# A transformer block's attention on 1 core: row tiles for scores and maxima, two head groups per sum, key masks made by GpSimd

## What is computed

```python
scores = einsum('bqhd,bkhd->bhqk', q, k) * 8 ** -0.5
out = einsum('bhqk,bkhd->bqhd', softmax(scores, axis=-1), v)
```

## Time and profile before

| | us |
|---|---|
| median of 3 runs | 498.83 |
| the profiled execution | 499.31 |
| its span, first to last instruction | 497.5 |
| PE busy | 428.4 (86%) |
| DVE busy | 351.3 (71%) |
| ACT busy | 289.2 (58%) |
| POOL busy | 61.4 (12%) |
| first score matmul starts | 61.85 |

### The profile page before, as it was taken

One profiled execution on the slowest core, in us unless ns is written; L12 is line 12 of the kernel. 1 busy time (PEld: TensorE's weight loads), 2 busy tenths in 40 slices (PEclk: granted clock), 3 DMA queues, 4 the chain that ended last, 5 costly groups with the idle time before them and its releaser, 6 DMA issues.

```text
span 497.5 us, 10420 instructions
## 1 busy us (share of the span) xinstructions
PE 428.4 (86%) x3664; PEld 271.1 (54%) x3664; DVE 351.3 (71%) x938; ACT 289.2 (58%) x535; POOL 61.4 (12%) x74
## 2 busy tenths in 40 slices
PE   0466699999999989889979989999999998989886
PEld 0433355656666664555545545656566665746464
DVE  4979477888888973875966948997979895531331
ACT  1022177666666666476665575656566667677552
POOL 5711010103021210210011001010101102020130
PEclk9989599999999999999999999999999999999989
DMA  8727475552746543323425136256546463510001
GB/s 256 268 64 212 146 218 138 175 138 84 195 162 171 164 131 107 92 80 113 96 83 165 42 118 152 81 154 194 135 147 154 137 184 113 116 38 24 1 1 42
DMA packets 34410, 63.30 MB, mean 127 GB/s; under 512 B 5535, under 2 KB 9887, under 8 KB 34079
## 3 DMA queue, kind: packets, MB, share of 16 engines
q1 hardware_dynamic: 34071, 62.42, 43.7%
q10 hardware_dynamic: 288, 0.21, 0.1%
HBM read 31.81 MB, written 26.74 MB: 118 GB/s over the span
## 4 chain that ended last, share of the span: by engine, by line
PE 61%; DVE 21%; DMA 5%; issue 4%; ACT 3%; POOL 3%; SPq 2%; DVEq 0%; ACTq 0%
PE ps_max L910 10%; PE ps_ao L942 9%; PE ps_sc L930 9%; PE ps_misc L892 8%; DVE maxima L680 7%; PE ps_misc L987 5%; PE ps_misc L967 5%; PE ps_misc L950 4%; DVE xn L584 4%; PE ps_misc L854 4%; DVE stats L574 3%; PE ps_misc L973 3%; POOL rstd L739 2%; DMA Kd<-Kh 2%; PE ps_misc L899 2%
## 5 line engine op out<-in xcount | busy, mean ns | idle before, releaser
L680 DVE TENSOR_REDUCE maxima<-ps_max 128x4 f32<-128x512 f32 (+1 forms) x256 | 159.7, 665 | 54.7 <-PE ps_max L910 47.4
L824 ACT ACTIVATE PT<-ps_sc 128x512 f32<-128x512 f32 (+1 forms) x256 | 138.9, 596 | 66.9 <-PE ps_sc L930 65.3
L910 PE MATMUL ps_max<-Kd,Qh 128*128 128x512 f32 (+1 forms) x256 | 105.1, 479 | 15.0 <-DMA Kd<-Kh 9.7
L930 PE MATMUL ps_sc<-Qd,Ks 97*128 97x512 f32 (+1 forms) x256 | 93.5, 444 | 0.9 <-issue 0.9
L942 PE MATMUL ps_ao<-PT,V 120*9 120x128 f32 (+1 forms) x2048 | 80.0, 274 | 0.3
L910 PEld LDWEIGHTS ps_max<-Kd,Qh 128*128 128x128 f32 x256 | 44.5, 195 | 51.5 <-issue 19.6
L942 PEld LDWEIGHTS ps_ao<-PT,V 120*9 120x9 f32 (+1 forms) x2048 | 43.3, 90 | 38.2 <-issue 33.5
L736 POOL TENSOR_SCALAR vareps<-mv 128x4 f32<-128x4 f32 (+1 forms) x28 | 6.4, 229 | 414.8 <-DVE mv L577 414.8
L930 PEld LDWEIGHTS ps_sc<-Qd,Ks 97*128 97x128 f32 (+1 forms) x256 | 44.5, 187 | 17.1 <-issue 9.9
L811 ACT ACTIVATE xnT<-ps_misc,vec 128x128 f32<-128x128 f32 x80 | 30.1, 460 | 35.2 <-PE ps_misc L854 18.8
L892 PE MATMUL ps_misc<-xnT,W 128*128 128x512 f32 x72 | 37.8, 639 | 6.4 <-ACT xnT L811 6.4
(11 more groups left out here) (74 smaller groups left out, 441.6 us busy)
## 6 DMA issues: line engine op xcount, KB each, us to landing
Qd<-q_mem SPq DMA_DIRECT2D x128, 96.0 KB
k_mem<-Kh SPq DMA_DIRECT2D x16, 512.0 KB, 2.9
q_mem<-Qh SPq DMA_DIRECT2D x16, 512.0 KB, 2.9
Ks<-k_mem SPq DMA_DIRECT2D x8, 768.0 KB, 7.1
Ks<-k_mem SPq DMA_DIRECT2D x8, 720.0 KB, 6.6
k_mem<-Kl SPq DMA_DIRECT2D x16, 256.0 KB, 3.2
q_mem<-Ql SPq DMA_DIRECT2D x16, 256.0 KB, 3.3
Kd<-Kh SPq DMA_DIRECT2D x128, 16.0 KB
```

What stands on the lines that cost most here:

```text
L680: dve.tensor_reduce(dst, ps_max[:, st.k % MAX_BANKS, 0:HG * ns].rearrange("p (h k) -> p h k", h=HG), AX_X, ALU.max, negate=True).then_inc( ...
L824: act.activation(PT[0:ns, st.k % 4, :], ps_sc[0:ns, st.k % 2, :], ACT.Exp, scale=SCALE).then_inc(S["probs_ready"], 1)
L910: pe.matmul(ps_max[:, st.k % MAX_BANKS, 0:HG * ns], Qh[:, st.f % 2, st.b * P:(st.b + 1) * P], Kd[:, HG * st.n:HG * st.n + HG, st.b * ns:(s ...
L930: pe.matmul(ps_sc[0:ns, st.k % 2, :], Ks[:, st.f % 2, st.n, st.b * ns:(st.b + 1) * ns], Qd[:, half % 3, st.n % GP, :, st.b * P:(st.b + 1) ...
```

## The change

- **Maxima** go by batch: one step makes the scores of the four head groups with four matmuls of 32 rows and 512 (480) columns, one in each row tile. `Kd[:, c]` holds the keys with the rows of the c-th head of every group, the rest zero, and has two slots. POOL makes it with four multiplications of `Kh` by a column of ones and zeros (`head_rows`, which DVE makes once with a sum over the identity); the DMAs and memsets of `Kd` are gone. `ps_max` is gone: the four products take four banks of `ps_misc`, now of 5 banks. The maxima of a unit are turned by one transpose in place of four.
- **Scores** go by two cells (groups 2g and 2g+1 of a batch): `Ks` and `Qd` have four blocks of 32 rows (24, a row for the maximum, 7 unused). Each row tile of 64 rows holds two heads; its matmul has 57 rows and 256 columns. Four such matmuls fill both banks of `ps_sc`, one for each row tile, so PE waits before each step until the exponentials of the step before are done (`probs_ready`, `GP * st.k`). `Qd` has two slots of a unit. ACT takes two exponentials of 512 columns for a step, as before.
- **Sums** of the two cells go to the same 128 columns: weights of 18 columns, with the head's values in the first 9 for the even group and in the last 9 for the odd, added up. A bank holds the sums of half a unit: 2 copies, 2 groups of 4 transposes, 2 reciprocals (of 32 in place of 16 elements) and 4 multiplications (of 128 in place of 64) for a unit.
- **Loads**: the keys come with 4 DMAs in place of 1, the queries with 4 in place of 8 (of twice the size), the maxima with 4 in place of 2.
- **Memsets** on POOL: `V` 3456 elements for each row in place of 1728, and its ones; `Ks` and two of `Qd`, of 4096 each, in place of four of 4096. DVE waits for the constants (`small_in`) before its first statistics.
- **The table `T`** is changed throughout: the first norm at -36.9 in place of -41.92, `value` (4.0, 3.57, 4.26, 5.04) in place of (2.15, 2.16, 2.1, 2.55), and so on. `EARLY` is [0.82, -3.59, -1.1, 0.1] in place of [-0.6, 1.18, 0.4, 0].

```diff
-SROWS = HG * SR
+TROWS = 32
+E = 2
+PAIRS = NG // 2 * CB
 FF = 4
-BANKS = 3
-MAX_BANKS = 2
+BANKS = 5
+ROWS = HG * HD
 VW = HD + 1
+PAIR = 2 * VW
+VSLOTS = 3
+PSLOTS = 4
...
-        for h in range(H):
-            at(t + T["kmask"][a] + h // HG * T["kstep"][a], Step("kmask", h=h, **who))
-        for i in range(period):
-            at(t + T["max"][a] + i // 2 * 2 * T["mstep"][a], Step("max", n=i // CB, b=i % CB, **who))
+        at(t + T["kmask"][a], Step("kmask", **who))
+        for b in range(CB):
+            at(t + T["max"][a] + NG * b * T["mstep"][a], Step("max", b=b, **who))
...
+        for i, (g, b) in enumerate(pairs):
+            at(t + 2 * i, Step("score", b=b, g=g, **who))
+            at(t + i // 2 * 4 + T["value"][a], Step("value", b=b, g=g, **who))
+        for g in range(GP):
+            at(t + 2 * CB * (g + 1) + T["copy"][a], Step("copy", g=g, **who))
+            at(t + 2 * CB * (g + 1) + T["norm"][a], Step("norm", g=g, **who))
...
-        Kd = sb("Kd", [P, H, CT], F32R)
-
-
-        Ks = sb("Ks", [SROWS + 1, 2, NG, CT], F32R)
-        Qd = sb("Qd", [SROWS + 1, 3, GP, HG, CT], F32R)
-        V = sb("V", [P, 3, CB, H, VW])
-        maxima = sb("maxima", [P, CB, H])
-        maxT = sb("maxT", [H, CT], F32R)
-        PT = sb("PT", [P, 4, CT])
...
+        Kd = sb("Kd", [P, 2, HG, CT], F32R)
+        head_rows = sb("head_rows", [P, HG])
+        Ks = sb("Ks", [P, 2, NG, CT], F32R)
+        Qd = sb("Qd", [P, 2, NG, E, CT], F32R)
+        V = sb("V", [P, VSLOTS, CB, H, PAIR])
+        maxima = sb("maxima", [P, H, CB])
+        maxT = sb("maxT", [H * CB, P], F32R)
+        PT = sb("PT", [P, PSLOTS, GP, GP, E, P])
...
-        ps_max = ctx.enter_context(nc.psum_tensor("ps_max", [P, MAX_BANKS, CT], F32))
...
-                        sp.dma_start(f32(Kd[r, st.h, 0:n]),
-                                     f32(Kh[r, st.f % 2, 0:n])).then_inc(S[f"kd_in{st.h // HG}"], 16)
...
-                        sp.dma_start(f32(Ks[0:SROWS, st.f % 2, :, 0:n]),
-                                     k_mem[st.f].rearrange("(n r) s t -> (r s) n t", n=NG)[:, :, 0:n]
-                                     ).then_inc(S[f"keys_in{st.f % 2}"], 16)
...
+                        heads = k_mem[st.f].rearrange("(n c r) s t -> c (r s) n t", n=NG, c=HG)
+                        for c in range(HG):
+                            sp.dma_start(f32(Ks[TROWS * c:TROWS * c + SR, st.f % 2, :, 0:n]),
+                                         heads[c][:, :, 0:n]).then_inc(S[f"keys_in{st.f % 2}"], 16)
...
+                            sp.dma_start(f32(Qd[TROWS * c:TROWS * c + SR, st.f % 2, :, c % E, :]),
+                                         heads[c]).then_inc(S[f"queries_in{st.f % 2}"], 16)
...
+                        heads = m_mem[st.f].rearrange("(n c a) t -> c a n t", n=NG, c=HG)
+                        for c in range(HG):
+                            row = TROWS * c + SR
+                            sp.dma_start(f32(Qd[row:row + 1, st.f % 2, :, c % E, :]),
+                                         heads[c]).then_inc(S[f"maxima_in{st.f % 2}"], 16)
...
+                dve.wait_ge(S["small_in"], 48)
+                dve.tensor_reduce(head_rows[:, :], ident.rearrange("p (n c d) -> p c n d", n=NG, c=HG), AX_XY,
+                                  ALU.add).then_inc(S["rows_ready"], 1)
...
-                            for g in range(2):
-                                dve.memset(f32(Kd[:, g * GH:(g + 1) * GH, :]), 0.0).then_inc(S["zeros_ready"], 1)
-                                if g == 0:
-                                    modulation()
+                            modulation()
...
-                        dve.wait_ge(S["max_scores"], st.k + 1)
-                        dst = maxima[:, st.b, HG * st.n:HG * st.n + HG]
-                        if st.n == 0 and st.b == 0 and st.f:
+                        if st.b == 0 and st.f:
                             dve.wait_ge(S["misc_filled"], mT_use[st.f - 1] + 1)
-                        dve.tensor_reduce(dst, ps_max[:, st.k % MAX_BANKS, 0:HG * ns].rearrange(
-                            "p (h k) -> p h k", h=HG), AX_X, ALU.max, negate=True).then_inc(S["max_taken"], 1)
+                        for n in range(NG):
+                            dve.wait_ge(S["misc_filled"], st.use + n + 1)
+                            dve.tensor_reduce(maxima[:, HG * n:HG * n + HG, st.b],
+                                              bank(st.use + n)[:, 0:HG * ns].rearrange("p (h k) -> p h k", h=HG),
+                                              AX_X, ALU.max, negate=True).then_inc(S["max_taken"], 1)
                     elif st.kind == "norm":
...
-                fill(1, V[:, :, :, :, :], 1.0)
+                fill(1, V[:, :, :, :, :], 0.0)
+                fill(2, V[:, :, :, :, HD:VW], 1.0)
...
-                            fill(2, f32(Qd[0:SROWS, 0, :, :, :]), 0.0)
-                            fill(3, f32(Ks[SROWS:SROWS + 1, :, :, :]), 1.0)
-                            fill(4, f32(Qd[0:SROWS, 1, :, :, :]), 0.0)
-                            fill(5, f32(Qd[0:SROWS, 2, :, :, :]), 0.0)
+                            fill(3, f32(Ks[:, :, :, :]), 1.0)
+                            for half in range(2):
+                                fill(4 + half, f32(Qd[:, half, :, :, :]), 0.0)
+                    elif st.kind == "kmask":
+
+                        n = CB * ns_of(st)
+                        pool.wait_ge(S["k_high"], st.f + 1)
+                        if st.f == 0:
+                            pool.wait_ge(S["rows_ready"], 1)
+                        if st.f >= 2:
+                            pool.wait_ge(S["max_taken"], GROUPS * (st.f - 1))
+                        for c in range(HG):
+                            pool.tensor_scalar(Kd[:, st.f % 2, c, 0:n], f32(Kh[:, st.f % 2, 0:n]),
+                                               head_rows[:, c:c + 1], None, ALU.mult).then_inc(S["kd_ready"], 1)
...
-                        act.wait_ge(S["scores_ready"], st.k + 1)
-                        if st.k >= 4:
-                            act.wait_ge(S["values_done"], st.k - 3)
-                        act.activation(PT[0:ns, st.k % 4, :], ps_sc[0:ns, st.k % 2, :], ACT.Exp,
-                                       scale=SCALE).then_inc(S["probs_ready"], 1)
+                        if st.k >= PSLOTS:
+                            act.wait_ge(S["values_done"], st.k - PSLOTS + 1)
+                        for g in range(GP):
+                            act.wait_ge(S[f"scores_ready{g}"], st.k + 1)
+                            act.activation(PT[0:ns, st.k % PSLOTS, g, :, :, :].rearrange("p i e t -> p (i e t)"),
+                                           ps_sc[0:ns, g, :], ACT.Exp, scale=SCALE).then_inc(S["probs_ready"], 1)
...
-                            pe.wait_ge(S[f"kd_in{st.n}"], 16 * HG * (st.f + 1))
-                        if st.b == 0 and st.n == 0:
+                            pe.wait_ge(S["kd_ready"], HG * (st.f + 1))
                             pe.wait_ge(S["q_high"], st.f + 1)
-                        if st.k >= MAX_BANKS:
-                            pe.wait_ge(S["max_taken"], st.k - MAX_BANKS + 1)
-                        pe.matmul(ps_max[:, st.k % MAX_BANKS, 0:HG * ns], Qh[:, st.f % 2, st.b * P:(st.b + 1) * P],
-                                  Kd[:, HG * st.n:HG * st.n + HG, st.b * ns:(st.b + 1) * ns],
-                                  start=True, stop=True).then_inc(S["max_scores"], 1)
+                        for n in range(NG):
+                            rows = slice(ROWS * n, ROWS * n + ROWS)
+                            fill(st.use + n)
+                            pe.matmul(bank(st.use + n)[:, 0:HG * ns], Qh[rows, st.f % 2, st.b * P:(st.b + 1) * P],
+                                      Kd[rows, st.f % 2, :, st.b * ns:(st.b + 1) * ns],
+                                      start=True, stop=True).then_inc(S["misc_filled"], 1)
                     elif st.kind == "mT":
...
-                        for b in range(CB):
-                            last = pe.transpose(bank(st.use)[0:H, b * P:(b + 1) * P], maxima[:, b, :], ident)
-                        last.then_inc(S["misc_filled"], 1)
+                        pe.transpose(bank(st.use)[0:CB * H, 0:P], maxima[:, :, :].rearrange("p h b -> p (h b)"),
+                                     ident).then_inc(S["misc_filled"], 1)
...
-                        if st.k >= 2:
-                            pe.wait_ge(S["probs_ready"], st.k - 1)
-                        pe.matmul(ps_sc[0:ns, st.k % 2, :], Ks[:, st.f % 2, st.n, st.b * ns:(st.b + 1) * ns],
-                                  Qd[:, half % 3, st.n % GP, :, st.b * P:(st.b + 1) * P],
-                                  start=True, stop=True).then_inc(S["scores_ready"], 1)
...
+                        if st.k:
+                            pe.wait_ge(S["probs_ready"], GP * st.k)
+                        for i in range(GP):
+                            n = GP * st.g + i
+                            for side in range(GP):
```

(64 more changed lines are left out.)

172 lines of the change are left out of this document (61 added, 111 removed).

## The result

The changed kernel takes 484.99 us (median of 4 runs, 484.4 to 485.76) against 499.12 us for the kernel before in the same session: ratio 0.971 (95% interval 0.967 to 0.974), 14 us faster. The forecast was 441, with a range of 410 to 472: the direction is right, the gain is a quarter of the one forecast, and the time lies outside the range. The profiled execution took 484.73 us, its span 482.9. Of one experiment (e9) half of the runs, the profiled one among them, fell in a slower state at a lower granted clock; its time is that of the others.

A forecast was written before the change was run, and what follows sets the result against it. The prediction took PE to bound the middle and a chain of latencies the head. Head 52, middle 358 and tail 30.5 gave 440.5, plus 1.8 between span and execution, minus 0.5: 441 us, range 410 to 472.

The forecast's parts named there:

- the price of a score step: PE's four score products, two at a time, take 0.45 us in place of 0.56; 14 us saved.
- The sums of DVE and ACT: Busy time in the middle: DVE from 299 to 290 us, ACT from 267 to 243 us.
- The head: Before the first score matmul: it starts at 52 us (48 to 60) in place of 61.85.
- PE's sum: PE's busy time in the middle falls from 377 to 308 us, bounds 277 and 367.
- Four maxima: A batch's four maxima products on PE take 0.55 us in place of 1.08; 32 us saved in the middle.
- The other products of PE: Norm transposes save 17 us and maxima transposes 6; the sums change by zero, at worst cost 13 us.
- The first (row tiles bring little): Maxima and scores on PE expose pipeline or don't overlap; PE stays bound, 465 to 485 us, chance 0.15.
- The drain that was weighed as a rule: A change of tiling mode drains TensorE, and the change makes two more modes; by it alone about 470 us.
- The fourth (slower, PE in `fill` behind DVE): PE waits before maxima until DVE's reductions have read the banks; 505 to 525 us, chance 0.04.
- the second (the chain of scores and exponentials, 455 to 468): Score, exponentials, score decides the middle; sign: PE idle 3 us or more a unit before scores; chance 0.17.
- The mask's term: POOL's masks cost 0.9 us each (0.5 to 1.3), 3.6 a unit, off PE's path; DVE is charged 5 us.
- How full: PE 86% busy over the whole middle in place of 93%: 358 us, 22.4 for a unit.

The follow-up runs named there:

- e9: The changed kernel with the score products alone on the first 64 rows, maxima still on four row tiles; 0.986 of the kernel before, 492.5 us.
- e5: The changed kernel with both GpSimd's reordered masks of e1 and the eleven pairs of filler matmuls of e2; 462.82 us.
- e3: The changed kernel with all maxima products on the first 32 rows and all score products on the first 64, so no row tiles; 531.09 us.
- e1: The changed kernel with only GpSimd's order changed: masks of units 1, 8, 9 and 10 wholly or partly behind the next norm's last step; 472.07 us.
- e2: The changed kernel with two unused filler matmuls before PE waits for the normalised input, in eleven of the 24 norms; 470.83 us.
- e15: e5 with the identity in place of both gelu functions, so that 12 of ACT's 13 table loads go; 462.93 us.
- e13: e5 with one filler matmul in place of two at each of the eleven norms; 465.93 us.
- e11: e5 with each half of a score step waiting only for its own bank's exponentials, one row tile after the other; 462.56 us.
- e7: e5 with the four MLP products of 512 columns spread over the score steps as in the kernel before; 485.25 us.
- e10: e5 with the sums of the first and second attention one score step later; 477.80 us.

## Why the prediction was wrong

**Right.** That row tiles run side by side, and the price of a score step: 0.43 us against 0.45. Half the copies and transposes. The sums of DVE and ACT (291 and 247 against 290 and 243). The gain of the units without MLP, 12%, with DVE 96% busy. The head came at 55.6 against 52, within its 48 to 60. PE's sum too, as far as it can be said: e5's middle has 333 us, of which the fillers are 15 and the lower level's part (some 18 us of records at half the rate) at most 9; that leaves 309 against the forecast 308.

**Right with luck.** PE's sum holds although its parts don't. Four maxima cost 0.42 to 0.44 us and not 0.55: the forecast took the four loads "one after the other", 0.43 us, where they run side by side in 0.19. That alone is some 8 us too much over 64 batches. Counted in the trace from each record's start to the next one's, e5's middle has 31 us for the maxima in place of 74, and 59 for the scores in place of 81: 43 and 22 us saved, not 32 and 14. The other products of PE, which were to lose 23, come to about as much as before once the clock's part is taken off; why isn't worked out.

**The rivals.** The first (row tiles bring little) is refuted by e3 and by the prices. The drain that was weighed as a rule beside it shows nowhere: the scores start 0.42 us behind four maxima, and the sums 0.43 behind the scores, less than the forecast had without a drain. The fourth (slower, PE in `fill` behind DVE) isn't seen: PE's idle time before the maxima with the reductions as releaser is 0.4 us in all. Of the second (the chain of scores and exponentials, 455 to 468) the sign was to be 3 us or more of PE's idle time a unit behind exponentials; it is 15.6 us in all, 1 a unit, in the changed kernel and in e5. Its range holds e5's time, which alone doesn't support it.

**The mask's term, mis-sized and misplaced.** The step "I take 0.9 (one tensor in, one out), 3.6 us for a unit", "Off PE's path, since a unit has a whole period for it", failed twice. The mask costs 1.58 us, 6.3 for a unit, outside the bounds that two nearest rows gave. And I asked only who waits for the masks, not what stands behind them on GpSimd: the last step of each norm (L744, L747), on which the stream's next stage waits. That is worth 13 us alone (e1), 8 when the clock is mended first (e5 against e2).

**The clock, a term that was left out.** I took every price from rows at the higher level and called the freed PE time a gain. In the earlier trace rows it stands at 1.00 in the middle and 0.88 in the head, where PE is half idle; that row was a sign that an emptier PE may not be granted the same clock, and I didn't read it. After, PE has stops before its transposes, and products behind them run at half the rate. That is worth 14 us alone (e2), 9 when the queueing is mended first (e5 against e1); both together 22 of the 44 us of the miss (e5).

**How full: one factor for two kinds of stretch.** 86% for PE, over a middle that has two regimes. Without MLP the second engine takes over, at 96%. With one, e5 still takes 32.7 us a unit against 33.7 before, PE 87% busy with its fillers (85.2 of 98.0 us), 78% without them (8.7 us). Before it was 89% (90.2 of 101.2). This is the rest of the miss: 376 us of middle in e5 where 358 was forecast, and 3 in the head. What sets those 33 us stays open. It isn't ACT's table loads (e15), nor PE's load alone (e13: about 1.4 us less work a unit gives 0.6 in two of the three units and nothing over the three together, 98.3 us), nor the missing half buffer by itself (e11). PE's waits in those three units of e5 are spread: 5.4 us for the copies of the normalised input (`xnT`), 4.2 for exponentials, 2.2 for other copies of ACT. That two small moves in the order cost 22 and 15 us (e7, e10) suggests that the in-order chain through PE, ACT and DVE decides there; that is argued, no run shows which link.

## What to carry to other kernels

When work is moved to an idle engine, list what already queues on it, and who waits for that: an engine that is a third busy can hold the critical step. When a change takes work off TensorE, its gain is only sure if it stays granted the higher clock; a few matmuls that compute nothing, put before a wait for another engine, can be worth more than they cost (14 us here for 22 of them), and 22 more cost nearly their full time (12 of 14 us). Forecast stretches with different bounds one by one, and cut the trace at the same unit before and after when they are compared.
